# Norms of layers 0 and 1 on GpSimd in two passes over whole rows, their ramp in ScalarE's copy of the turned rows

## The chip, the cores and the metric

The kernel runs on one core of a Trainium2 chip. The metric is the time of one execution on the device in microseconds (us). The kernel before was run three times: the median is 1065.44 us, the lowest 1063.51, the highest 1066.78.

## The reference, cut to what matters

Sixteen graphs of 512 nodes with 128 features each pass through four graph layers, each behind a layer norm without weights and a ramp, and each added to its input:

```python
h = jnp.maximum(_layernorm(x, axis=-1), 0.0)      # (x - m) / sqrt(v + eps), then max(., 0)
x = x + _L0_gnn_ref(h, adj, L0_gnn_W, L0_gnn_a)   # attention over neighbours, one head
h = jnp.maximum(_layernorm(x, axis=-1), 0.0)
x = x + _L1_gnn_ref(h, adj, L1_gnn_W, L1_gnn_b, L1_gnn_a)   # the same with four heads
h = jnp.maximum(_layernorm(x, axis=-1), 0.0)
x = x + _L2_gnn_ref(h, adj, a0, a1, a2, a3, bias)  # edge kinds, sigmoid of h * a * h'
h = jnp.maximum(_layernorm(x, axis=-1), 0.0)
x = x + _L3_gnn_ref(h, adj, weight, w_ih, w_hh, b_ih, b_hh) # three rounds of a gated unit
```

In layers 0 and 1 h is used only through products with weights, so only the turned form of it (features on the partitions) is needed. Layers 2 and 3 use h also as it stands.

## The kernel before, in words

All arrays of a graph lie in SBUF as 128 partitions by 4 blocks (C = 4) by 128 features; a tile of 128x512 floats is a whole graph. Every step of a graph has a name. A_STEPS are layer 0, L_STEPS layer 1 (16 units n, v, q: masked maximum, exponential, transposition), B_STEPS layer 2, C_STEPS the three rounds of layer 3. Several graphs are in work at once: while one is in layers 2 and 3, the next is in layer 0 or 1. Each engine takes its own list of (graph, step), sorted by written times: BEGIN has the start of each of the four groups of steps for each graph, WHEN an offset for each step and engine (`in_order`, line 133). The order within an engine is fixed by these tables, and semaphores join the engines. Each engine works in order, so an instruction that waits holds all behind it.

A layer norm n goes like this:

- VectorE takes the sums (bn_stats, line 623), the moments (line 629), the negated mean (line 634) and variance plus eps (line 636; line 638 for layer 3).
- GpSimd raises the latter to the power -0.5 (line 363) and multiplies it with the negated mean into `shift` (line 365), both on 128x4 floats.
- ScalarE writes hn = relu(rstd * x + shift), in four activations of 128x128 (line 394), one for each block, since scale and shift are one number for each partition and block.
- TensorE turns the four blocks into a PSUM bank (`turn_rows`, line 936) and ScalarE copies that bank into hT in one activation of 128x512 (`copy_hT`, line 399).

On GpSimd's queue stand besides these only the two loads of adj of each graph (lines 371 and 379). In the middle of the run its order is: mean1 of graph g, mean0 of graph g+1, mean2 of g, the two loads, mean3 of g.

Other lines that are spoken of: 642 and 663 (masked maximum and logits of a unit on VectorE, operands spread, mask and probs in SBUF), 678 and 730 (the two masks, from adj in bf16), 739 (values out of PSUM), 796 and 802 (x2: the scaled product out of PSUM, then the addition of x1, both operands in SBUF), 870 (r_t times hid_n, both in SBUF), 885 (the new state, turned by TensorE on line 1142), 441 (ScalarE counts edges), 476 (ScalarE's copy avT, turned by TensorE on line 1049).

## Time and profile before

| | |
|---|---|
| median of 3 runs | 1065.44 us (1063.51 to 1066.78) |
| the profiled execution | 1066.04 us, span 1063.9 us |
| busy, share of the span | PE 90%, DVE 84%, ACT 81%, POOL 12% |
| mean granted TensorE clock | 0.967 of full speed |
| the chain that ended last | PE 52%, DVE 28%, ACT 10%, waiting for nothing shown 6%, POOL 3% |

PE is TensorE (PEld its weight loads), DVE VectorE, ACT ScalarE, POOL GpSimd. A row of the timeline has the start in us from the start of the span, the duration in us, the engine, the line of the kernel, the operation, the tiles (out<-in) with their shapes, and how many instructions were merged; in brackets stands how long the engine was idle in front of it and what ended that. The chain of work that ended last is followed back from the last instruction: at each step to what released it, or to the instruction before it on its engine.

### The profile page before, as it was taken

The numbers are of one execution on the slowest core, as the hardware profiler recorded it, in microseconds if no ns is written. First come the engines' busy times: TensorE is split into PE (matmuls) and PEld (weight loads), VectorE is DVE, ScalarE is ACT, GpSimd is POOL, SyncE is SP. The second block draws the span as 40 slices with busy tenths as digits, with TensorE's granted clock in tenths as the row PEclk, the third lists the DMA queues.
The fourth block names the chain that finished last, engine by engine and source line by source line (L and its number), as shares of the span: only waits on it lengthen the run. The fifth ranks groups of instructions, "written<-read, shape, count | busy, mean of one in ns | idle before, by whom it ended". The sixth has DMA issues, their size and how long they took to land.

```text
span 1063.9 us, 16086 instructions
## 1 busy us (share of the span) xinstructions
PE 954.6 (90%) x5024; PEld 609.6 (57%) x5024; DVE 892.3 (84%) x2710; ACT 864.0 (81%) x1860; POOL 132.6 (12%) x170
## 2 busy tenths in 40 slices
PE   4588998999989899999989899998989999998866
PEld 3455565666566566656556566656656665655443
DVE  5296989899898979899897989989897989979543
ACT  3367888979888897988888897988889798887742
POOL 1102011010202011020201201020201101010000
PEclk8558999999999999999999999999999999999989
DMA  2401204021210403121220402121030302111000
GB/s 72 109 1 39 72 11 109 11 61 52 68 51 14 106 11 77 44 60 51 56 64 10 110 11 60 60 61 51 15 105 11 79 31 61 50 40 51 1 11 10
DMA packets 42477, 52.32 MB, mean 49 GB/s; under 512 B 1296, under 2 KB 25872, under 8 KB 42384
## 3 DMA queue, kind: packets, MB, share of 16 engines
q0 software_dynamic: 16896, 25.17, 10.7%
q1 hardware_dynamic: 17040, 21.83, 6.5%
q10 hardware_dynamic: 8448, 4.20, 1.3%
q8 instruction: 44, 0.72, 0.3%
q14 instruction: 49, 0.40, 0.1%
HBM read 55.39 MB, written 4.19 MB: 56 GB/s over the span
## 4 chain that ended last, share of the span: by engine, by line
PE 52%; DVE 28%; ACT 10%; issue 6%; POOL 3%; DMA 0%; DVEq 0%; SPq 0%; ACTq 0%; POOLq 0%
PE l_bank L948 7%; DVE probs L642 6%; PE a_bank L981 6%; PE x_bank L1040 4%; PE a_bank L948 3%; PE h_bank L1102 3%; ACT hn L394 3%; PE r_bank L1102 3%; PE r_bank L1105 3%; DVE sess L843 3%; DVE sess L836 3%; PE h_bank L1105 3%; PE n_bank L1105 3%; DVE probs L663 3%; POOL rstd L363 2%
## 5 line engine op out<-in xcount | busy, mean ns | idle before, releaser
L663 DVE SCALAR_TENSOR_TENSOR probs<-spread,s_lift,probs 128x512 f32<-128x512 f32 x320 | 237.4, 747 | 4.0 <-DVE rmax L642 0.5
L642 DVE CUSTOM_DVE_ANT_0 probs<-spread,mask 128x512 f32<-128x512 f32 x320 | 211.8, 684 | 2.4 <-ACT spread L450 2.3
L363 POOL TENSOR_TENSOR rstd<-var_eps,power 128x4 f32<-128x4 f32 x64 | 88.0, 1375 | 882.5 <-DVE var_eps L636 603.0
L460 ACT ACTIVATE probs<-probs,shift_p 128x512 f32<-128x512 f32 x256 | 185.7, 725 | 5.7 <-DVE shift_p L659 5.7
L468 ACT ACTIVATE pT<-l_bank 128x512 f32<-128x512 f32 x256 | 151.8, 600 | 46.5 <-PE l_bank L948 46.3
L948 PEld LDWEIGHTS l_bank<-ident,probs 128*128 128x128 f32 x1024 | 124.3, 144 | 73.8 <-issue 46.0
L948 PE MATMUL l_bank<-ident,probs 128*128 128x128 f32 x1024 | 150.5, 278 | 6.1 <-ACT probs L460 5.1
L394 ACT ACTIVATE hn<-x,shift,rstd 128x128 f32<-128x128 f32 x192 | 80.5, 492 | 26.1 <-POOL shift L365 26.0
L1005 PE MATMUL l_bank<-hT,dst_rep 128*128 128x512 f32 x128 | 73.6, 658 | 12.1 <-ACT pT L468 8.5
L870 DVE SCALAR_TENSOR_TENSOR hid_n<-r_t,hid_n 128x512 f32<-128x512 f32 x48 | 33.1, 689 | 57.8 <-ACT r_t L518 57.8
L981 PE MATMUL a_bank<-values,pT 128*128 128x128 f32 x512 | 65.7, 286 | 0.7 <-ACT pT L428 0.7
L1088 PE MATMUL y_bank<-hn,sess 128*128 128x128 f32 x512 | 61.6, 278 | 4.2 <-DVE sess L843 4.1
L1088 PEld LDWEIGHTS y_bank<-hn,sess 128*128 128x128 f32 x512 | 58.4, 192 | 11.9 <-DVE sess L843 11.9
L981 PEld LDWEIGHTS a_bank<-values,pT 128*128 128x128 f32 x512 | 63.0, 202 | 2.0 <-ACT pT L428 2.0
L1040 PE MATMUL x_bank<-pT,values 128*32 128x512 f32 x512 | 58.2, 595 | 0.7 <-ACT pT L468 0.7
L450 ACT ACTIVATE spread<-l_bank 128x512 f32<-128x512 f32 x64 | 38.4, 600 | 23.4 <-PE l_bank L1005 23.4
L948 PEld LDWEIGHTS a_bank<-ident,probs 128*128 128x128 f32 x256 | 29.9, 149 | 44.5 <-ACT pT L428 35.8
L948 PE MATMUL a_bank<-ident,probs 128*128 128x128 f32 x256 | 44.4, 300 | 9.7 <-ACT probs L423 5.6
L460 ACT ACTIVATION_READ_ACCUMULATOR probs<-probs,shift_p 128x1 f32 x256 | 51.8, 202 | 0.0
L1105 PE MATMUL r_bank<-aggT,gi_w 128*128 128x512 f32 x96 | 49.4, 596 | 0.0
L1105 PE MATMUL h_bank<-aggT,gi_w 128*128 128x512 f32 x96 | 49.1, 593 | 0.0
L1105 PE MATMUL n_bank<-aggT,gi_w 128*128 128x512 f32 x96 | 49.1, 593 | 0.0
(175 smaller groups left out, 1956.5 us busy)
## 6 DMA issues: line engine op xcount, KB each, us to landing
adjt_i<-in_adj_t SPq DMA_DIRECT2D x16, 1024.0 KB, 5.2
edges<-in_adj POOLq DMA_DIRECT2D x16, 1024.0 KB, 5.9
adj_h<-in_adj POOLq DMA_DIRECT2D x16, 512.0 KB, 7.7
xin<-in_x SPq DMA_DIRECT2D x16, 256.0 KB, 2.9
out<-out_sb ACTq DMA_DIRECT2D x16, 256.0 KB, 3.8
weights_sb<-in_weights SPq DMA_DIRECT2D x1, 840.0 KB, 4.7
```

The lines of the kernel that those rows point to most:

```text
L363: g.tensor_tensor(rstd[n][:], var_eps[n][:], power[:], op=ALU.pow).then_inc(pool_step[n], 1)
L394: s.activation(hn[n][:, c, :], rows[:, c, :], ACT.Relu, bias=shift[n][:, c:c + 1], scale=rstd[n][:, c:c + 1]).then_inc(hn_ready[n], 1)
L460: s.activation(row, row, ACT.Exp, bias=shift_p[:, head, c:c + 1], accum_out=den[:, head, c:c + 1]).then_inc(probs_ready, 1)
L468: s.activation(pT[:, head - 1, :, c * P:(c + 1) * P], l_banks[unit % 2][:, :].rearrange("p (j i) -> p j i", j=C), ACT.Copy).then_inc(pT_co ...
L642: return v.tensor_tensor_reduce(out=row, in0=spread_row, in1=mask, scale=1.0 / LIFT, scalar=-3e38, op0=ALU.subtract, op1=ALU.max, accum_ou ...
L663: v.scalar_tensor_tensor(row, spread_row, source, row, ALU.min, ALU.subtract, reverse1=True).then_inc(ready, 1)
L948: last = t.transpose(dst[:, j * P:(j + 1) * P], row[:, j * P:(j + 1) * P], ident[:])
L981: last = t.matmul(a_bank[:, c * P:(c + 1) * P], pT0[:, j, c * P:(c + 1) * P], values0[:, j, :], start=(j == 0), stop=(j == C - 1))
L1005: t.matmul(l_banks[head % 2][:, :], dst_rep[:, head, :], hT[1][:, :], start=True, stop=True).then_inc(dst_ready, 1)
L1040: last = t.matmul(x_bank[h * HD:(h + 1) * HD, :], values1[:, j, h * HD:(h + 1) * HD], pT[:, h, j, :], start=(j == 0), stop=(j == C - 1), s ...
L1088: last = t.matmul(y_bank[:, c * P:(c + 1) * P], sess[:, j, c * P:(c + 1) * P], hn[2][:, j, :], start=False, stop=(j == C - 1), skip_group_ ...
L1105: t.matmul(bank[:, :], gi_w[:, layer, gate * D:(gate + 1) * D], aggT[:, :], start=start, stop=True).then_inc(gi_ready, 1)
```

## The change

For layers 0 and 1 the normalization moves from ScalarE to GpSimd. GpSimd subtracts the mean from the whole 128x512 tile (the mean is read from `moments`, spread over each block's 128 features), waits for its own result, and multiplies the whole tile with rstd, spread in the same way. The ramp goes to the copy of the turned rows: `copy_hT` uses Relu in place of Copy for n < 2. For these two layers the negated mean on VectorE and the product for `shift` on GpSimd fall away, the step names norm0_0 to norm0_3 (norm1_0 to norm1_3) become one step norm0 (norm1), and `turn_rows` waits for one pass in place of four. GpSimd's new steps stand directly behind mean0 and mean1 of the same graph. The tables WHEN lose the entries of the steps that fell away; the order of all that stays is the same on every engine. Layers 2 and 3 are as before.

The diff, without the tables:

```diff
--- before.py
+++ after.py
@@ -20,9 +20,9 @@
 PLAIN = 1024.0
 
 
-A_STEPS = (["stats0", "aggr0", "mean0"] + [f"norm0_{c}" for c in range(4)] + ["rows0", "mask0", "dst0", "src0", "values0"] + [f"m{c}" for c in range(4)]
+A_STEPS = (["stats0", "aggr0", "mean0"] + ["norm0"] + ["rows0", "mask0", "dst0", "src0", "values0"] + [f"m{c}" for c in range(4)]
            + ["u0", "top0", "u1", "t0", "below0", "u2", "t1", "max0", "u3", "t2", "t3", "den0", "rden0"] + [f"sum0_{c}" for c in range(4)] + ["x1"])
-L_STEPS = (["stats1", "aggr1", "mean1"] + [f"norm1_{c}" for c in range(4)] + ["count", "rows1", "mask1", "dst1", "edges", "values1"]
+L_STEPS = (["stats1", "aggr1", "mean1"] + ["norm1"] + ["count", "rows1", "mask1", "dst1", "edges", "values1"]
            + [f"n{c}" for c in range(4)] + ["dst2"]
            + [step for n in range(16)
...
@@ -279,6 +276,7 @@
         stats_ready = [sem(f"stats_ready{n}") for n in range(NORMS)]
         pool_step = [sem(f"pool_step{n}") for n in range(NORMS)]
         ln_ready = [sem(f"ln_ready{n}") for n in range(NORMS)]
+        centred = [sem(f"centred{n}") for n in range(2)]
         hn_ready = [sem(f"hn_ready{n}") for n in range(NORMS)]
         hT_ready = [sem(f"hT_ready{n}") for n in range(NORMS)]
         hT_copied = [sem(f"hT_copied{n}") for n in range(NORMS)]
@@ -362,7 +360,18 @@
                 pool.wait_ge(stats_ready[n], p.count(1, 1))
                 g.tensor_tensor(rstd[n][:], var_eps[n][:], power[:], op=ALU.pow).then_inc(pool_step[n], 1)
                 pool.wait_ge(pool_step[n], p.count(1, 1))
-                g.tensor_tensor(shift[n][:], minus_mean[n][:], rstd[n][:], op=ALU.mult).then_inc(ln_ready[n], 1)
+                if n >= 2:
+                    g.tensor_tensor(shift[n][:], minus_mean[n][:], rstd[n][:], op=ALU.mult).then_inc(ln_ready[n], 1)
+
+            def norm(p, n, rows):
+
+                if p.before().exists():
+                    pool.wait_ge(hT_ready[n], p.before().count(1, 1))
+                g.tensor_tensor(hn[n][:, :, :], rows, moments[n][:, :, 0:1].to_broadcast([P, C, D]),
+                                op=ALU.subtract).then_inc(centred[n], 1)
+                pool.wait_ge(centred[n], p.count(1, 1))
+                g.tensor_tensor(hn[n][:, :, :], hn[n][:, :, :], rstd[n][:, :].unsqueeze(2).to_broadcast([P, C, D]),
+                                op=ALU.mult).then_inc(hn_ready[n], 1)
 
             def load_adj(p):
                 if p.before().exists():
@@ -379,6 +388,10 @@
                     g.dma_start(edges[:, p.graph % 2, :, :], rows(adj, p.graph)).then_inc(edges_loaded[p.graph % 2], 16)
                 if step[:4] == "mean":
                     deviation(p, int(step[4]))
+                if step == "norm0":
+                    norm(p, 0, xin[:, p.graph % 2, :, :])
+                if step == "norm1":
+                    norm(p, 1, x1[:, p.graph % 2, :, :])
 
             load_adj(Place(0))
             for graph, step in in_order("gpsimd", G):
@@ -396,13 +409,11 @@
 
             def copy_hT(p, n, src):
                 act.wait_ge(hT_ready[n], p.count(1, 1))
-                s.activation(hT[n][:, :], src[:, :], ACT.Copy).then_inc(hT_copied[n], 1)
+                s.activation(hT[n][:, :], src[:, :], ACT.Relu if n < 2 else ACT.Copy).then_inc(hT_copied[n], 1)
 
             def step_a(p, step):
                 prev = p.before()
-                if step[:5] == "norm0":
-                    norm(p, 0, int(step[6]), xin[:, p.graph % 2, :, :])
-                elif step == "rows0":
+                if step == "rows0":
                     copy_hT(p, 0, a_bank)
                 elif step == "dst0":
                     act.wait_ge(dst0_ready, p.count(1, 1))
@@ -430,9 +441,7 @@
 
             def step_l(p, step):
                 prev = p.before()
-                if step[:5] == "norm1":
-                    norm(p, 1, int(step[6]), x1[:, p.graph % 2, :, :])
-                elif step == "rows1":
+                if step == "rows1":
                     copy_hT(p, 1, l_bank0)
                 elif step == "count":
                     act.wait_ge(adj_loaded, p.count(16, 16))
@@ -631,7 +640,8 @@
 
             def deviation_of(n, chain):
                 chain.wait()
-                v.tensor_scalar(minus_mean[n][:, :], moments[n][:, :, 0], -1.0, None, ALU.mult)
+                if n >= 2:
+                    v.tensor_scalar(minus_mean[n][:, :], moments[n][:, :, 0], -1.0, None, ALU.mult)
                 if n < NORMS - 1:
                     last = v.tensor_scalar(var_eps[n][:, :], moments[n][:, :, 1], EPS, None, ALU.add)
                 else:
@@ -931,7 +941,8 @@
                     t.matmul(bk[:, 0:3 * D], gate_wt_sb[i], w_iht_sb[:], start=True, stop=True).then_inc(pe_w, 1)
 
             def turn_rows(p, n, dst):
-                pe.wait_ge(hn_ready[n], p.count(C, C))
+                passes = C if n >= 2 else 1
+                pe.wait_ge(hn_ready[n], p.count(passes, passes))
                 for c in range(C):
                     last = t.transpose(dst[:, c * P:(c + 1) * P], hn[n][:, c, :], ident[:])
                 last.then_inc(hT_ready[n], 1)
```

## Rows read from the trace of the kernel before

**Rows 1.** The page, busy us (share of the span) and instructions by engine.
```profile
PE 954.6 (90%) x5024; PEld 609.6 (57%) x5024; DVE 892.3 (84%) x2710; ACT 864.0 (81%) x1860; POOL 132.6 (12%) x170
```

**Rows 2.** Busy time by stretch: A, then B; columns in the first line.
```profile
core 0: us, PE busy (x) PEld busy (x) DVE busy (x) ACT busy (x) POOL busy (x), PEclk, DMA share, GB/s
398.00:424.10 26.10, 23.96 (x121) 15.72 (x120) 25.68 (x79) 20.12 (x44) 3.51 (x5) 1.00 0.30 66
424.10:458.65 34.55, 33.31 (x196) 21.05 (x195) 29.25 (x89) 33.38 (x74) 5.72 (x6) 1.00 0.13 43
```

**Rows 3.** Waits, 205.8 to 874.1 us: total us, times, longest.
```profile
DVE hid_n L870 <- ACT r_t L518: 28.6, 11, 3.2
...
PE x_bank L936 <- ACT hn L394: 9.7, 13, 0.8
```

**Rows 4.** Groups of instructions: busy us, mean ns, idle us before them.
```profile
L394 ACT ACTIVATE hn<-xin,shift,rstd 128x128 f32<-128x128 f32 x64 | 26.2, 482 | 4.7 <-POOL shift L365 4.7
```

**Rows 5.** Timeline of one period, 448 to 466 us, all engines.
```profile
448.75 1.01 POOL L363 TENSOR_TENSOR rstd<-var_eps,power 128x4 f32<-128x4 f32 x1 [22.84 <-DVE var_eps L636]
...
451.71 0.69 DVE L870 SCALAR_TENSOR_TENSOR hid_n<-r_t,hid_n 128x512 f32<-128x512 f32 x1 [3.04 <-ACT r_t L518]
...
452.44 1.66 ACT L394 ACTIVATE hn<-x,shift,rstd 128x128 f32<-128x128 f32 x4
...
454.40 2.58 POOL L363 TENSOR_TENSOR rstd<-var_eps,power 128x4 f32<-128x4 f32 x1 [4.36 <-DVE var_eps L636]
...
456.15 0.69 DVE L885 SCALAR_TENSOR_TENSOR state<-keep,n_t 128x512 f32<-128x512 f32 x1
...
456.92 0.66 PE L936 MATMUL l_bank<-ident,hn 128*128 128x128 f32 x4
...
457.42 0.60 PE L1142 MATMUL h_bank<-ident,state 128*128 128x128 f32 x4
...
459.38 0.69 DVE L802 TENSOR_TENSOR x<-x 128x512 f32<-128x512 f32 x1
...
459.94 1.64 ACT L394 ACTIVATE hn<-xin,shift,rstd 128x128 f32<-128x128 f32 x4
...
463.50 1.38 POOL L363 TENSOR_TENSOR rstd<-var_eps,power 128x4 f32<-128x4 f32 x1 [6.24 <-DVE var_eps L636]
...
464.80 0.60 PE L936 MATMUL a_bank<-ident,hn 128*128 128x128 f32 x4
```

**Rows 6.** Groups of instructions on GpSimd: fills and the select.
```profile
L358 POOL TENSOR_SCALAR_AFFINE_SELECT ident<-ident 128x128 f32<-128x128 f32 x1 | 0.3, 287 | 0.2 <-POOL ones_h L356 0.2
...
L353 POOL MEMSET ident<- 128x128 f32 x1 | 0.2, 202 | 0.0
...
L354 POOL MEMSET power<- 128x4 f32 x1 | 0.1, 98 | 0.0
```

**Rows 7.** Timeline, GpSimd beside three VectorE instructions, two places.
```profile
40.64 0.86 DVE L623 BATCH_NORM_STATS2 stats<-xin 128x6 f32<-128x128 f32 x4
40.81 1.01 POOL L363 TENSOR_TENSOR rstd<-var_eps,power 128x4 f32<-128x4 f32 x1 [34.13 <-DVE var_eps L636]
...
41.84 0.66 DVE L730 TENSOR_SCALAR mask<-adj_h 128x2048 bf16<-128x2048 bf16 x1
41.91 0.65 POOL L365 TENSOR_TENSOR shift<-minus_mean,rstd 128x4 f32<-128x4 f32 x1
...
100.74 0.42 DVE L739 TENSOR_TENSOR values<-l_bank,b_rows 128x256 f32<-128x256 f32 x1
100.91 1.01 POOL L363 TENSOR_TENSOR rstd<-var_eps,power 128x4 f32<-128x4 f32 x1 [6.52 <-DVE var_eps L636]
```

**Rows 8.** Timeline, a period of the other kind, 576 to 583 us.
```profile
578.21 1.38 POOL L363 TENSOR_TENSOR rstd<-var_eps,power 128x4 f32<-128x4 f32 x1 [6.19 <-DVE var_eps L636]
...
581.33 0.69 DVE L802 TENSOR_TENSOR x<-x 128x512 f32<-128x512 f32 x1
```

**Rows 9.** Timeline, norm 1 of the first graph, 40 to 47 us.
```profile
44.38 1.09 PE L936 MATMUL l_bank<-ident,hn 128*128 128x128 f32 x4 [6.47 <-ACT hn L394]
...
46.13 0.57 ACT L399 ACTIVATE hT<-l_bank 128x512 f32<-128x512 f32 x1
```

131 rows, old and new, of the table WHEN are left out of this document.

## Prediction

> **What bounds the kernel now.** I read the page's totals first. TensorE is busy for 90% of the span, VectorE for 84%, ScalarE for 81% and GpSimd for 12% [rows 1]. So the idle engine is the one that gets the work, but the share alone doesn't say what relief on ScalarE is worth. For that I read a table by stretch. In the middle of the run one graph leaves every 60.8 us (mean of 13 periods, 145.8 to 936.2 us), and each period falls into two stretches. Stretch A runs from the addition that makes x2 (line 796) to the variance of layer 3: 26.10 us, of which VectorE is busy 25.68. Stretch B is the rest: 34.55 us, TensorE busy 33.31, ScalarE 33.38, VectorE only 29.25 [rows 2]. The chain of work that ended last has VectorE in A and TensorE in B, and four more periods look alike. So a period is VectorE's work in A plus TensorE's work in B. ScalarE is very busy in B, but it is TensorE that has no gap there: of its 1.24 idle us, about 0.9 is the wait for the rows of layer 3's norm (9.7 us in 11 periods [rows 3]), which the change doesn't touch.
>
> **What is removed.** On ScalarE 128 activations of 128x128 at about 0.48 us each [rows 4], each started before the one in front of it ends: the four of norm 1 take 1.66 us at the end of B, and the four of norm 0 1.64 near the start of A [rows 5]. Norm 1 is done at 454.1 us and its transposes start at 456.92; norm 0 is done at 461.6 and its transposes start at 464.80 [rows 5]. TensorE waits for neither in the steady periods. What is behind them on ScalarE (gate activations, the count, the copies of avT and hT) comes at most a fraction earlier, since it waits for TensorE, which is full. Gain: at most 1.24 - 0.9, some 0.4 us a period, if all waits of B went, 5 us in 13; I take 0.1 a period, 1 us. On VectorE 32 small instructions (minus_mean) go, all in B, where VectorE waits anyway (28.6 us in 11 periods for r_t [rows 3]): nothing. GpSimd's product for shift goes, 32 times 0.2 us or a little more. The copy of the turned rows keeps its instruction with another function: taken as nothing, as both kinds read the same bank; if it cost 0.1 us more the copy for layer 1 would have to be paid, 1.6 us at most.
>
> **What is added: the price of a pass.** GpSimd gets 64 passes over 128x512 floats, each reading two operands. No row of before shows one. GpSimd fills 128x128 in 0.202 us and 128x4 in 0.098, which is 0.84 ns an element of a row for a write; the affine select, which reads once and writes once, takes 0.287 for 128 elements, 1.52 ns [rows 6]. A read is thus about 0.68 ns, and two reads and a write about 2.2 ns: 0.2 + 508 x 2.2 = 1.32 us a pass. Lower end: both operands at the price of one, 0.2 + 508 x 1.52 = 0.97. Upper end: the whole price twice, 1.75. I take 1.32, the sum of the parts. The two passes with their two hand-overs of 0.08 end 2.80 us after the power.
>
> The Trainium skill has a price of its own (GPSIMD Engine Reference, section 3.1): a two-input pass over 2048 floats takes 4497 ns. By it I would estimate 1.2 to 1.3 us for 512, and a sum about 1 us lower; no row here shows it.
>
> **Do they come in time?** Norm 1: the power ends at 449.76, the passes at 452.56, or 0.7 later if a VectorE instruction cuts in; the transposes start at 456.92. Norm 0: the power ends at 456.98, the passes at 459.8; the transposes start at 464.80 [rows 5]. Both earlier than ScalarE delivers now. Behind norm 1 on GpSimd's queue stands the power of the next graph's norm 0, four or more us later; behind norm 0 the power of layer 2, at 463.50 [rows 5], and only then the two loads of adj. None of them is moved.
>
> **What they collide with.** The power reads four elements of two tiles. Beside bn_stats (one operand from SBUF) it takes 1.01 us, and beside line 739 (one operand from PSUM) also 1.01. The shift product, 0.20 us alone, takes 0.65 when the mask of line 730 runs in front of it, and so ends just after that mask [rows 7]. The power at 454.40 takes 2.58: VectorE works through a mask and instructions with two SBUF operands without a gap, and GpSimd gets in only before the last [rows 5]. So GpSimd stands still while VectorE runs a mask or two SBUF operands. That VectorE stands still when GpSimd is the first, no row shows: GpSimd's reads of four elements are too short. I take it that the block holds both ways, and for the whole pass.
>
> The Trainium skill says so (SBUF — State Buffer, section "Who interferes with whom"): the pair of ports that VectorE and GpSimd share is an exclusive lock, and "whoever issues first" holds it for the whole instruction. The trace agrees with the half in which VectorE is first; for the other half it is silent.
>
> Place 1, in A, where VectorE is the bound. The addition of line 802 reads x1 and x2 from SBUF. In front of it the power for norm 0 ends at 456.98 and it starts at 459.38, 2.40 us later [rows 5]; in the other kind of period 579.59 and 581.33, 1.74 us later [rows 8]. Read in the same way, 7 of the 13 periods have 2.36 to 2.41 and 6 have 1.51 to 1.88. The second pass starts 1.48 after the power, mostly ahead of the addition, and ends at 2.80: it holds VectorE for 0.40 us in each of the seven, 2.8 us, and for 1.1 on average in the six, 6.6 us. Together 9.4. The 0.4 us a period by which VectorE isn't busy in A [rows 2] may swallow some: I take 0.25 a period, 3 us. Left: 6.4.
>
> Place 2, in B. Line 870 (r_t and hid_n, both in SBUF) starts 0.9 to 2.16 us after the power of norm 1, 1.95 in the period shown (449.76 to 451.71). Eight times it meets the first pass for 0.2 to 0.5 us, five times the second for 0.6 to 0.9. What hides it is the slack of the state: made at 456.84, read by TensorE at 457.42 [rows 5], 0.58 us less a hand-over of 0.05. Only the five go over, by some 0.3: 1.5 us.
>
> Place 3, the first graph. TensorE waits 6.47 us for norm 1, which starts at 44.38 [rows 9]. The first pass waits for the mask until 42.50, and the two passes end at 45.2, some 0.9 late. But the copy behind the transposes starts only at 46.13, since it stands behind the count on ScalarE, and the count now runs 1.6 us earlier; the copy then starts at about 46.45. That is 0.3; with the constants of VectorE at 6 to 10 us, which norm 0 may hold up to 1 us, I take 0.7.
>
> **The sum.** 6.4 + 1.5 + 0.7 - 1.0 = +7.6 us. The profiled execution has 1066.04 us, 2.14 beyond its span of 1063.9, and gives 1073.6; it lies 0.6 above the median of 1065.44. On the median: 1073.0 us. With a pass of 0.97 the two are over before the addition in the seven and cost 2.3 us in the six, which A swallows: 1065. With 1.75 it meets the addition by 1.25 us in seven periods, and the first pass alone reaches it in the six; line 870 goes over the slack in most periods, some 8 us: together +18, 1084.
>
> **Rivals.**
> - VectorE isn't held: it wins every time, or GpSimd's reads slip between its instructions. For it: no VectorE instruction of before is stretched beside GpSimd. Against: none ever stood behind a long read. Then only the 1 us of relief and 0.7 at the start are left: 1065.
> - The relief on ScalarE counts: it is as full as TensorE in B [rows 2], and with 1.66 us a period less in its queue what follows could reach TensorE sooner. Against: TensorE's waits for ScalarE in B are small. At most 0.4 a period: 1060.
> - The pass holds VectorE in places that I count as free, slower than forecast: it costs 1.75 us, or also stops instructions with one SBUF operand. The place is the same, lines 796 to 802 at the head of A; it decides from a pass of about 1.5 us on. 1084.
> - The forecast itself is slower than before; the point from which it bites is (2.40 - 0.16) / 2 = 1.12 us a pass in the seven periods, 0.8 in the six.
>
> **Chances.** Forecast 0.53, VectorE not held 0.26, relief counts 0.12, heavy case 0.09. A measurement of this kernel tells 0.3% (3.2 us) from no change. Faster by over that: 0.11, most of the relief case. Within: 0.31, the unheld case with the low end of the forecast. Slower: 0.58. The range leaves out the best of the relief case and the end of the heavy one: 1062 to 1083.
>
> **What would show it.** Right: GpSimd's passes at 1.2 to 1.4 us where VectorE is silent; line 802, 0.69 us now, at 1.1 to 1.8 or starting late after line 796; line 870 the same in some periods; stretch A longer by 0.3 to 1 us, B by less than 0.3; TensorE's and ScalarE's spans in B as they are. Wrong: line 802 stays at 0.69 and A at 26 us (VectorE isn't held), or B shrinks with ScalarE (relief). Wrong too if a transposition of norm 0 or 1 waits for GpSimd, or if the power of layer 2 starts late.

## The result and the profile after

The changed kernel takes 1067.89 us, the median of 13 runs (1066.74 to 1070.35), against 1065.49 for 13 runs of the kernel before: a ratio of 1.0027, 95% interval 1.0018 to 1.0036. It is 2.4 us slower, where 7.6 was forecast. The profiled execution took 1067.27 us, with a span of 1065.5.

The page's totals of the kernel after, to be read against [rows 1]:

```profile
PE 948.3 (89%) x5008; PEld 606.6 (57%) x5024; DVE 900.0 (84%) x2678; ACT 818.7 (77%) x1732; POOL 191.9 (18%) x202
```

ScalarE lost 45.3 us of work and GpSimd gained 59.3. VectorE has 32 instructions fewer and yet is busy 7.7 us longer. That is the trail to follow.

Stretches A and B of one period, as in [rows 2] (same columns):

```profile
399.17:424.99 25.82, 23.44 (x117) 15.44 (x117) 25.39 (x77) 18.30 (x40) 4.37 (x5) 1.00 0.27 65
424.99:459.72 34.73, 33.48 (x198) 21.35 (x198) 29.49 (x89) 32.48 (x70) 8.85 (x8) 1.00 0.14 44
```

A is no longer than before, B is. In this period A went from 26.10 to 25.82 and B from 34.55 to 34.73. Over the 13 periods the sum of A went from 336.82 to 336.77 and that of B from 453.14 to 454.56.

GpSimd's groups in the kernel after (busy us, mean ns), and the spread of one of them (minimum, median, maximum in ns):

```profile
L373 POOL TENSOR_TENSOR hn<-hn,rstd 128x512 f32<-128x512 f32 x32 | 35.4, 1105 | 2.5
L370 POOL TENSOR_TENSOR hn<-x,moments 128x512 f32<-128x512 f32 x16 | 17.1, 1072 | 1.3
```
```profile
L370 POOL TENSOR_TENSOR hn<-xin,moments x16: 1042/1044/1161, 6.1 to 885.5; 128x512 f32<-128x512 f32 x16
```

A pass is 1.04 us where nothing disturbs it, not 1.32. Longer ones are those that VectorE itself stops, as at 43.12 us below.

Line 870 is now 880, 802 is 812, 885 is 895, 1142 is 1153, 796 is 806, 363 is 361, 936 is 947, 399 is 412, 476 is 485, 1049 is 1060. Durations of two lines of VectorE in the kernel after; before, no instruction of either took more than 0.693 us:

```profile
L880 DVE SCALAR_TENSOR_TENSOR hid_n<-r_t,hid_n x48: 679/692/1559, 136.0 to 1056.8; 128x512 f32<-128x512 f32 x48
...
L812 DVE TENSOR_TENSOR x<-x x16: 679/692/1214, 99.4 to 1004.5; 128x512 f32<-128x512 f32 x16
```

The timeline of one period of the kernel after, 389 to 401 us, to be read against [rows 5]:

```profile
389.48 1.01 POOL L361 TENSOR_TENSOR rstd<-var_eps,power 128x4 f32<-128x4 f32 x1 [23.50 <-DVE var_eps L646]
...
390.56 1.04 POOL L370 TENSOR_TENSOR hn<-x,moments 128x512 f32<-128x512 f32 x1
...
391.68 1.04 POOL L373 TENSOR_TENSOR hn<-hn,rstd 128x512 f32<-128x512 f32 x1
391.77 1.50 DVE L880 SCALAR_TENSOR_TENSOR hid_n<-r_t,hid_n 128x512 f32<-128x512 f32 x1 [2.37 <-ACT r_t L527]
...
395.20 2.58 POOL L361 TENSOR_TENSOR rstd<-var_eps,power 128x4 f32<-128x4 f32 x1 [2.47 <-DVE var_eps L646]
...
396.95 0.69 DVE L895 SCALAR_TENSOR_TENSOR state<-keep,n_t 128x512 f32<-128x512 f32 x1
...
396.98 0.66 PE L947 MATMUL l_bank<-ident,hn 128*128 128x128 f32 x4
...
397.69 0.66 PE L1153 MATMUL h_bank<-ident,state 128*128 128x128 f32 x4
397.86 1.05 POOL L370 TENSOR_TENSOR hn<-xin,moments 128x512 f32<-128x512 f32 x1
...
398.99 1.04 POOL L373 TENSOR_TENSOR hn<-hn,rstd 128x512 f32<-128x512 f32 x1
399.17 0.69 DVE L806 TENSOR_TENSOR x<-y_bank,rden 128x512 f32<-128x512 f32 x1 [1.53 <-PE y_bank L1060]
...
399.90 0.69 DVE L812 TENSOR_TENSOR x<-x 128x512 f32<-128x512 f32 x1
```

Three readings. Line 880 starts just behind the second pass of norm 1 and takes 1.50 us: it gets going only when that pass is over. The state then ends at 397.64, and TensorE turns it at 397.69, 0.71 us behind the turn of norm 1 (0.50 in [rows 5], and 0.49 in this very period of the kernel before), so it waited 0.2 us. And the passes of norm 0 end at 400.03, hardly later than line 812 starts (399.90), which keeps its 0.69.

The other kind of period, to be read against [rows 8]:

```profile
579.26 1.38 POOL L361 TENSOR_TENSOR rstd<-var_eps,power 128x4 f32<-128x4 f32 x1 [4.38 <-DVE var_eps L646]
...
580.72 1.04 POOL L370 TENSOR_TENSOR hn<-xin,moments 128x512 f32<-128x512 f32 x1
...
581.85 1.04 POOL L373 TENSOR_TENSOR hn<-hn,rstd 128x512 f32<-128x512 f32 x1
582.36 1.07 DVE L812 TENSOR_TENSOR x<-x 128x512 f32<-128x512 f32 x1
```

Here the addition starts 1.72 us after the power's end and is held for 0.38. Only two of the 13 periods show it by more than 0.05 us (0.38 and 0.52).

Two more places matter in B. In the first, norm 0's pass gets in ahead of the instruction that makes the state (line 895) and holds it for 0.73 us. In the second, line 880 had been held for 0.87, and the delay travels through ScalarE: its n_t gate waits 0.58 us for VectorE's hid_n, the count stands behind the gate, the copy avT (line 485) behind the count, and TensorE turns avT on line 1060:

```profile
334.91 1.16 POOL L370 TENSOR_TENSOR hn<-xin,moments 128x512 f32<-128x512 f32 x1
...
335.21 1.42 DVE L895 SCALAR_TENSOR_TENSOR state<-keep,n_t 128x512 f32<-128x512 f32 x1
```
```profile
760.34 0.72 ACT L535 ACTIVATE n_t<-hid_n,gate_b 128x512 f32<-128x512 f32 x1 [0.58 <-DVE hid_n L884]
...
762.96 0.57 ACT L485 ACTIVATE avT<-x_bank 128x512 f32<-128x512 f32 x1
...
763.68 0.63 PE L1060 MATMUL y_bank<-ident,avT 128*128 128x128 f32 x4
```

The first graph, whose start the change touches twice. In the kernel before the four copies of the constants took 0.68 us and the first transposes started at 9.53:

```profile
6.06 1.04 POOL L370 TENSOR_TENSOR hn<-xin,moments 128x512 f32<-128x512 f32 x1
...
6.66 1.76 DVE L591 COPY a_heads<-weights_sb 32x2 f32<-32x2 f32 x4
7.18 1.04 POOL L373 TENSOR_TENSOR hn<-hn,rstd 128x512 f32<-128x512 f32 x1
...
11.15 1.06 PE L947 MATMUL a_bank<-ident,hn 128*128 128x128 f32 x4
```

And its norm 1, to be read against [rows 9]:

```profile
43.06 0.66 DVE L740 TENSOR_SCALAR mask<-adj_h 128x2048 bf16<-128x2048 bf16 x1
43.12 1.49 POOL L370 TENSOR_TENSOR hn<-x,moments 128x512 f32<-128x512 f32 x1
43.63 1.01 DVE L646 TENSOR_SCALAR var_eps<-moments 128x4 f32<-128x4 f32 x1
44.70 1.04 POOL L373 TENSOR_TENSOR hn<-hn,rstd 128x512 f32<-128x512 f32 x1
...
45.88 1.08 PE L947 MATMUL l_bank<-ident,hn 128*128 128x128 f32 x4 [6.69 <-POOL hn L373]
...
47.00 0.60 ACT L412 ACTIVATE hT<-l_bank 128x512 f32<-128x512 f32 x1 [12.47 <-PE l_bank L947]
```

Both sides of the block stand in these lines. The pass at 43.12 is long (1.49) because the mask is in front of it; then VectorE's 128x4 instruction at 43.63, 0.16 us else, takes 1.01 because the pass is in front of that.

### The profile page after: what moved, and what is told of

Its sections match the earlier page's. It is cut to its first block, busy times and chain, and to the rows that moved or that the text cites. A ratio compares the mean times of both kernels' runs of the same rounds, so it can differ in the third digit from the quotient of the medians.

```text
span 1065.5 us, 15972 instructions
## 1 busy us (share of the span) xinstructions
PE 948.3 (89%) x5008; PEld 606.6 (57%) x5024; DVE 900.0 (84%) x2678; ACT 818.7 (77%) x1732; POOL 191.9 (18%) x202
## 4 chain that ended last, share of the span: by engine, by line
PE 48%; DVE 32%; ACT 10%; issue 6%; POOL 3%; DMA 0%; DVEq 0%; SPq 0%; ACTq 0%; POOLq 0%
DVE probs L652 7%; PE a_bank L992 6%; PE l_bank L959 6%; PE x_bank L1051 4%; PE a_bank L959 3%; PE h_bank L1113 3%; DVE probs L673 3%; DVE sess L846 3%; PE r_bank L1113 3%; DVE sess L853 3%; DVE stats L632 3%; PE r_bank L1116 3%; PE h_bank L1116 2%; PE n_bank L1116 2%; ACT hn L407 2%
## 5 line engine op out<-in xcount | busy, mean ns | idle before, releaser
L361 POOL TENSOR_TENSOR rstd<-var_eps,power 128x4 f32<-128x4 f32 x64 | 84.0, 1313 | 824.7 <-DVE var_eps L646 546.9
L469 ACT ACTIVATE probs<-probs,shift_p 128x512 f32<-128x512 f32 x256 | 185.7, 725 | 5.9 <-DVE shift_p L669 5.9
L880 DVE SCALAR_TENSOR_TENSOR hid_n<-r_t,hid_n 128x512 f32<-128x512 f32 x48 | 38.5, 801 | 58.6 <-ACT r_t L527 58.6
L407 ACT ACTIVATE hn<-x,shift,rstd 128x128 f32<-128x128 f32 x128 | 53.4, 483 | 17.1 <-POOL shift L364 17.1
L520 ACT ACTIVATE aggT<-n_bank 128x512 f32<-128x512 f32 x32 | 19.1, 598 | 53.0 <-PE n_bank L1131 53.0
L434 ACT ACTIVATE probs<-probs,shift_p 128x512 f32<-128x512 f32 x64 | 46.3, 731 | 4.4 <-DVE shift_p L669 4.4
```

The lines of the kernel that those rows point to most:

```text
L361: g.tensor_tensor(rstd[n][:], var_eps[n][:], power[:], op=ALU.pow).then_inc(pool_step[n], 1)
L407: s.activation(hn[n][:, c, :], rows[:, c, :], ACT.Relu, bias=shift[n][:, c:c + 1], scale=rstd[n][:, c:c + 1]).then_inc(hn_ready[n], 1)
L469: s.activation(row, row, ACT.Exp, bias=shift_p[:, head, c:c + 1], accum_out=den[:, head, c:c + 1]).then_inc(probs_ready, 1)
```

## The experiments

The theory is the prediction's: a pass holds every VectorE instruction with two SBUF operands that comes behind it, in three places. Rivals: VectorE isn't held at all; the loss comes from the start alone; the relief of ScalarE is what moves the time. Here are all kernels in one table. "First x2" is the start of line 796 for the first graph, A and B are summed over the 13 periods, "tail" runs from the end of layer 3's variance of the last graph to the end of the last arithmetic instruction (the span goes on for 2.3 us, for the store of the result); these come from one profile each. "Held" is the time over 0.69 us, with its count, of line 802 and of line 870. Medians and ratios are against the kernel before in the same series.

| kernel | first x2 | A | B | tail | 802 held | 870 held | median (before) | ratio, 95% |
|---|---|---|---|---|---|---|---|---|
| before | 97.82 | 336.82 | 453.14 | 39.15 | 0 | 0 | 1065.49 | |
| after | 98.69 | 336.77 | 454.56 | 38.75 | 0.95 (3) | 5.42 (10) | 1067.89 (1065.49) | 1.0027, 1.0018 to 1.0036 |
| relief_only | 92.05 | 336.33 | 452.49 | 42.42 | 0 | 0 | 1059.80 (1065.86) | 0.9941, 0.9929 to 0.9954 |
| passes_only | 99.01 | 339.00 | 453.26 | 42.38 | 4.00 (10) | 2.67 (10) | 1068.37 (1065.86) | 1.0031, 1.0013 to 1.0049 |
| fills_only | 96.90 | 335.82 | 452.95 | 39.07 | 0 | 0 | 1068.49 (1065.86) | 1.0020, 1.0002 to 1.0037 |
| norm0_only | 99.03 | 337.82 | 453.31 | 40.50 | 1.91 (6) | 0 | 1069.28 (1065.86) | 1.0028, 1.0017 to 1.0038 |
| norm1_only | 96.47 | 336.42 | 453.88 | 38.96 | 0 | 5.41 (10) | 1064.47 (1064.01) | 0.9998, 0.9988 to 1.0009 |
| third_pass | 97.93 | 339.63 | 454.01 | 38.78 | 4.57 (8) | 5.42 (10) | 1071.80 (1064.01) | 1.0075, 1.006 to 1.009 |
| after_add | 98.61 | 337.66 | 453.85 | 42.37 | 0 | 5.47 (10) | 1072.59 (1064.01) | 1.0072, 1.0058 to 1.0086 |
| one_operand | 96.43 | 336.27 | 452.60 | 43.50 | 0 | 0 | 1064.86 (1064.01) | 1.0004, 0.9995 to 1.0014 |
| graph0_scalar | 98.16 | 337.17 | 454.97 | 42.93 | 0.90 (2) | 5.27 (9) | 1069.44 (1065.61) | 1.0033, 1.0015 to 1.005 |
| graph0_one_operand | 94.40 | 337.22 | 452.89 | 40.44 | 0 | 0 | 1065.31 (1065.61) | 0.9998, 0.9987 to 1.001 |
| third_pass_norm1 | 98.69 | 336.99 | 454.39 | 39.92 | 1.43 (4) | 5.51 (10) | 1070.38 (1065.61) | 1.005, 1.0033 to 1.0068 |
| by_block | 96.02 | 336.82 | 452.57 | 43.57 | 1.15 (9) | 1.76 (11) | 1068.00 (1065.61) | 1.0012, 0.9999 to 1.0025 |
| before_again | 98.00 | 336.76 | 453.08 | 39.11 | 0 | 0 | 1066.11, one run | |
| after_again | 98.05 | 336.90 | 454.37 | 40.44 | 0.95 (3) | 5.43 (10) | 1068.60, one run | |

How far can a column be trusted? The last two rows repeat the two kernels:

> The kernel before, profiled once more. Theory (what differs between executions of one kernel is the granted clock before 150 us and in the last 40, not the steady part): the 13 periods from 155 to 945 us sum to 790.0 us within 0.5; the start up to the first addition of x2 and the stretch behind the last norm may differ by 1 to 3 us with the clock. Rival (the steady part itself moves by 1 us or more from execution to execution, so the sums say nothing): a sum off by 1 us or more.

> The changed kernel, profiled once more. Theory: the 13 periods sum to 791.3 us within 0.5, 1.4 over before, with line 870's held instructions at 5.4 us in all and line 802's at 0.9; start and end go with the clock. Rival: the sum is off by 1 us or more and the held instructions lie elsewhere.

The sum A + B is 789.96 and 789.84 before, 791.33 and 791.27 after: the same within 0.12 us, so the 13 periods cost 1.4 us, and the held instructions repeat too. The first x2 moves by up to 0.6 us and the tail by 1.7 between executions of one kernel. The steady stretch is read from these sums; the ends of the span only by their mechanism, and medians that differ by 3 us or less with care. This caution is needed: of the twelve altered kernels, only passes_only and third_pass_norm1 have a median inside the range that the theory gave in advance. third_pass and one_operand miss it by up to 0.2 us, the other eight by 1 us or more. What follows therefore goes by the sums over the periods and by the held instructions.

### The two halves of the change

**relief_only.** TensorE turns the rows as they are; the norms fall away:

```diff
-            def norm(p, n, rows):
...
-                    last = t.transpose(dst[:, c * P:(c + 1) * P], hn[n][:, c, :], ident[:])
+                    rows = (xin, x1)[n][:, p.graph % 2] if n < 2 else hn[n]
+                    last = t.transpose(dst[:, c * P:(c + 1) * P], rows[:, c, :], ident[:])
```

> The changed kernel without its 32 pairs of passes: norms 0 and 1 are left out (TensorE turns the rows as they are once the power is there), the ramp stays in the copy. Theory (the passes hold VectorE, relief on ScalarE is worth nothing): 1064 to 1066 us, stretch B as long as before. Rival 1 (the relief is worth 3 us or more and the passes cost twice what shows): 1060 to 1062 us. Rival 2 (all of the loss is at the start, VectorE's constants held by norm 0 of graph 0): 1064 to 1066 as well, but then the periods of the changed kernel are as long as these.

The median fell by 6 us, more than any case foresaw. In the profile the first x2 is 5.8 us earlier, since the first graph, where all engines wait for it, has no norms to wait for. In the 13 periods A lost 0.49 and B 0.65: the relief is 1.1 us. The rival that relief counts has no more than that to live on, and this kernel, not before, is the base for what the passes cost: A + 0.44 and B + 2.07 in the kernel after.

**passes_only.** The kernel before, with the same two passes into a tile that nobody reads:

```diff
+            def passes(p, n, rows):
+                wide = extra[:, :].rearrange("p (c d) -> p c d", c=C)
...
+                g.tensor_tensor(wide, rows, moments[n][:, :, 0:1].to_broadcast([P, C, D]),
+                                op=ALU.subtract).then_inc(centred[n], 1)
+                pool.wait_ge(centred[n], p.count(1, 1))
+                g.tensor_tensor(wide, wide, rstd[n][:, :].unsqueeze(2).to_broadcast([P, C, D]),
+                                op=ALU.mult).then_inc(scaled_ready[n], 1)
```

> The kernel before with the 32 pairs of passes added on GpSimd, into a tile that nobody reads; ScalarE keeps its norms. Theory: the loss of the change, 2 to 4 us over before, with line 870 and a few others stretched by up to 0.9 us. Rival 1: 5 us or more over before, since the relief is missing. Rival 2: 1 to 2 us, all of it before 100 us.

No engine reads what these passes write. Only guards against overwriting wait for passes of earlier graphs, and the profile shows no such wait but two of loads of x, for neither of which VectorE then waits. Still the kernel is slower. Line 802 is held in 10 of its 16, 4.0 us in all; A grows by 2.18. Here shift's product comes first, so the passes end some 0.14 us later, and the gaps between the power and line 802 are close to those that the prediction read: 1.51 to 1.87 in six periods, 2.05 to 2.36 in seven. The place and the mechanism are as forecast; the size hangs on tenths of a microsecond. That A grows by 1.8 less than the holds looks like the part that A was to swallow, but it isn't an even 0.25 a period: of the four largest holds (0.74, 0.65, 0.51 and 0.47) the periods grew by 0.43, 0.86, 0.51 and 0.04.

**fills_only.** The same, with two writes of the same length that read nothing:

```diff
-                g.tensor_tensor(wide, rows, moments[n][:, :, 0:1].to_broadcast([P, C, D]),
-                                op=ALU.subtract).then_inc(centred[n], 1)
+                g.memset(wide, 1.0).then_inc(centred[n], 1)
```

> As the kernel with passes added, but each pass is a fill of 1.04 us that reads nothing. Theory (it is GpSimd's reads that hold VectorE's second SBUF operand): line 870 and line 802 stay at 0.69 us and the time at before's, 1065 to 1066; only VectorE's masks and copies may still be held. Rival (GpSimd holds VectorE whatever it does): as with the passes, 2 to 4 us over before.

Groups and timeline of fills_only:

```profile
L379 POOL MEMSET fills<- 128x1128 bf16 x32 | 33.7, 1052 | 1.9
...
L826 DVE TENSOR_TENSOR x<-x 128x512 f32<-128x512 f32 x16 | 11.0, 689 | 0.4
```
```profile
6.55 2.51 DVE L601 COPY a_heads<-weights_sb 32x2 f32<-32x2 f32 x4
...
701.01 1.04 POOL L379 MEMSET fills<- 128x1128 bf16 x1
...
701.21 0.69 DVE L826 TENSOR_TENSOR x<-x 128x512 f32<-128x512 f32 x1
```

GpSimd is as busy as with the passes, but neither line is held, and A + B is 1.2 us below before (why below, I can't say). Line 802 starts within a fill 6 times, with up to 0.83 us of it left, and line 870 14 times, with up to 0.51 left; none takes over 0.69. A GpSimd that is merely busy and writes thus doesn't hold them: it takes a pass that reads. Some instructions with one operand are held by a fill also: the constants' copies take 2.51 us, a 128x4 one 1.07, and one mask 1.50 in place of 0.69. The median doesn't follow the sums: the 12 runs fall into two groups, 1063.2 to 1064.5 and 1068.5 to 1070.7. What makes the groups isn't in the 13 periods of the profile that I have, which is of a run of the lower group. passes_only and graph0_scalar fall into two groups in the same way (1066.1 to 1068.9 and 1071.8 to 1074.4; 1064.3 to 1066.0 and 1069.1 to 1073.1), so a median there depends on how many runs fell into each.

**norm0_only** and **norm1_only.** The change for one of the two layers, the other as before:

```diff
-                g.tensor_tensor(shift[n][:], minus_mean[n][:], rstd[n][:], op=ALU.mult).then_inc(ln_ready[n], 1)
+                if n != 0:
+                    g.tensor_tensor(shift[n][:], minus_mean[n][:], rstd[n][:], op=ALU.mult).then_inc(ln_ready[n], 1)
...
+                if step == "mean0":
+                    whole(p, 0, xin[:, p.graph % 2, :, :])
```

> Only norm 0 is moved to GpSimd, norm 1 stays on ScalarE. Theory: the start costs 0.9 us, place 1 (line 802 in A) almost nothing since a pass takes 1.04 us and not 1.32: 1066 to 1067 us. Forecast's view (place 1 carries most): 1067 to 1068 and norm 1 alone would cost nothing.

> Only norm 1 is moved to GpSimd, norm 0 stays on ScalarE. Theory: line 870 is held by up to 0.9 us as in the changed kernel, and of that about 1 us in 13 periods goes over the slack of the state in B; A stays; the start loses some 0.5 us. 1066 to 1068 us. Rival (the two norms' costs add up to the change's): 1065 us, since norm 0 alone already costs about all of it.

The medians are again of little help: norm0_only is 2.3 us above the range expected, norm1_only 1.5 below. With norm 0 alone A grows by 1.0 and B by 0.17, six additions are held; with norm 1 alone A loses 0.4 and B gains 0.74, ten of line 870 are held. One hold of each kernel shows how close this is. Norm0_only:

```profile
154.13 1.38 POOL L364 TENSOR_TENSOR rstd<-var_eps,power 128x4 f32<-128x4 f32 x1 [5.82 <-DVE var_eps L648]
155.59 1.04 POOL L372 TENSOR_TENSOR hn<-xin,moments 128x512 f32<-128x512 f32 x1
156.72 1.04 POOL L375 TENSOR_TENSOR hn<-hn,rstd 128x512 f32<-128x512 f32 x1
...
157.36 0.95 DVE L814 TENSOR_TENSOR x<-x 128x512 f32<-128x512 f32 x1
```

The gap from the power's end (155.51) to the addition is 1.85 us, and 0.26 is lost. The six gaps 1.58, 1.66, 1.80, 1.84, 1.85 and 1.95 go with 0.52, 0.44, 0.29, 0.25, 0.26 and 0.15: 2.11 less the gap within 0.03 each time. In the kernel after, where norm 1 holds line 870 as well, the same periods have 1.57, 2.05, 1.72, 2.31, 2.30 and 2.40, and only three are held. So moving norm 1 too takes holds away from norm 0's passes: three of the six gaps grew beyond the point from which it bites, and a fourth nearly to it. It isn't the delay of line 870 that does this. In relief_only nothing is held, and the same periods, in the same order, have 2.02, 2.05, 2.31, 2.31, 2.31 and 2.40 (one_operand within 0.04); in passes_only line 870 is held while ScalarE keeps its norms, and they have 1.51 to 1.87. What moves the gaps is that norm 1 leaves ScalarE (and with it go its negated mean on VectorE and its shift on GpSimd). Its passes, as far as the comparison goes, work the other way: with them two of the six are back at 1.57 and 1.72, and these two are the ones that pay in the kernel after. Norm1_only shows the same with norm 0 on ScalarE: 1.50 and 1.64 there, 1.98 to 2.33 in the other four.

In sum over the periods, A and B together, norm 0 costs 1.2, norm 1 0.3 and both 1.4, with the relief in each; only the share of A and B is another (A + 1.0 and - 0.4 alone, 0 together).

### The dose

**third_pass.** One more pass ahead of norm 0's two:

```diff
+                if n == 0:
+                    g.tensor_tensor(extra[:, :, :], rows, moments[n][:, :, 0:1].to_broadcast([P, C, D]),
+                                    op=ALU.subtract).then_inc(extra_done, 1)
+                    pool.wait_ge(extra_done, p.count(1, 1))
```

> The changed kernel with a third pass in front of norm 0's two, into a tile that nobody reads: the passes end 3.25 us after the power and not 2.1. Theory (line 802 is held exactly as long as a pass still runs when it comes): in the 7 periods with a gap of 2.3 to 3.8 us it is held by up to 1 us, in the others by what is left of the second pass, and A grows by 0.3 to 0.7 us a period, 4 to 8 us over the changed kernel: 1072 to 1076. Rival (VectorE's gaps in A swallow it): below 1070.

A is 2.86 us longer than in the kernel after, B 0.55 shorter, and line 802 is held 4.57 us in place of 0.95. The median is 7.8 us over before, of which the periods hold 3.7. One period of third_pass shows why the periods don't lose more:

```profile
396.51 2.58 POOL L363 TENSOR_TENSOR rstd<-var_eps,power 128x4 f32<-128x4 f32 x1 [2.48 <-DVE var_eps L652]
...
399.17 1.04 POOL L373 TENSOR_TENSOR extra<-xin,moments 128x512 f32<-128x512 f32 x1
...
400.29 1.04 POOL L376 TENSOR_TENSOR hn<-xin,moments 128x512 f32<-128x512 f32 x1
...
401.21 0.69 DVE L818 TENSOR_TENSOR x<-x 128x512 f32<-128x512 f32 x1
...
401.41 1.39 POOL L379 TENSOR_TENSOR hn<-hn,rstd 128x512 f32<-128x512 f32 x1
```

The addition comes in the seam between two passes, goes first, and the third pass waits (1.39 for 1.04). So the point isn't how long the norm lasts but in which pass the addition falls.

**third_pass_norm1.** The same line with `if n == 1`.

> The changed kernel with a third pass in front of norm 1's two. Theory (the slack of the state is 0.5 us, one held instruction costs what goes over it): line 870 is held in nearly every period by 0.3 to 0.9 us, as now; the five periods in which it came after the passes now pay too, and norm 0's power comes later against line 802: 0 to 3 us over the changed kernel, far less than norm 0's third pass (A grew by 2.9 us): 1068 to 1071. Rival (a pass costs the same wherever it stands): 1072 or more.

Line 870 is held 5.51 us against 5.42, and A + B is 791.38 against 791.33: line 870 meets the second of three passes where it met the second of two, and starts 0.07 us behind it (0.09 in the kernel after). A further pass behind the one that holds costs nothing here. The median is 4.8 us over before, and that is not in the periods: in the profile the tail is 1.2 longer than in the kernel after, and the rest isn't accounted for.

**after_add.** Norm 0's passes wait for the addition:

```diff
+                if n == 0 and p.before(2).exists():
+                    pool.wait_ge(x2_ready, p.before(2).count(1, 1))
```

> The changed kernel, but norm 0's passes wait for the addition of line 802 of the graph in layer 2. Theory: line 802 is back at 0.69 us everywhere, the passes lie beside bn_stats and operands from PSUM, the transposes of norm 0 still don't wait; A is shorter by what two held additions cost, 0.5 to 1 us: 1066.5 to 1067.5. Rival (the two held additions were no cost in the period): as the changed kernel, 1067.9. Rival 2 (norm 0 now comes too late for its transposes): 1070 or more.

The median, 1072.59, is as high as rival 2 has it, but not for its reason: no transposition of norm 0 waits. Line 802 is free, but A is 0.9 longer than in the kernel after and A + B the same (791.51). The passes now fall on the masked maxima, of which seven are held for 1.86 us; before, all of them took at most 0.69. The hold was moved, not removed. That the median is 4.7 over that of the kernel after isn't in the periods either; the tail of this profile is 3.6 longer.

**one_operand.** Each norm in four instructions with both numbers as scalars, so that only one operand is a row:

```diff
-                g.tensor_tensor(hn[n][:, :, :], rows, moments[n][:, :, 0:1].to_broadcast([P, C, D]),
-                                op=ALU.subtract).then_inc(centred[n], 1)
...
+                for c in range(C):
+                    last = g.tensor_scalar(hn[n][:, c, :], rows[:, c, :], moments[n][:, c, 0:1], rstd[n][:, c:c + 1],
+                                           ALU.subtract, ALU.mult)
```

> The changed kernel, but GpSimd makes a norm in four instructions of 128x128, each (row - mean) * rstd with two scalars of a partition, so one operand of 512 elements is read in place of two times two. Theory: some 0.3 us an instruction, 1.2 us a norm in place of 2.1; line 870 and line 802 are held for 0.3 us at most: 1065 to 1066 us, and the start loses less. Rival (an instruction costs by its start, 0.5 us or more): 2 us a norm and no gain, 1067 to 1068.

One_operand's own GpSimd instructions, and its addition beside them:

```profile
L371 POOL TENSOR_SCALAR hn<-xin,moments,rstd x64: 790/798/1333, 6.2 to 883.2; 128x128 f32<-128x128 f32 x64
```
```profile
395.38 2.87 POOL L371 TENSOR_SCALAR hn<-xin,moments,rstd 128x128 f32<-128x128 f32 x3
...
396.88 0.71 DVE L811 TENSOR_TENSOR x<-x 128x512 f32<-128x512 f32 x1
```

An instruction takes 0.79 us where 0.3 was expected, so a norm lasts 3.2 us and more, longer than two passes, and lies across the addition. Lines 802 and 870 start within such an instruction 26 times, with up to 1.21 us of it left, and none is lengthened by more than 0.02. One state is held for 0.14 us, and at the start two tiny instructions for 0.2 together. A + B is 788.87, 1.1 below before, and A and B each within 0.12 of relief_only: that is the relief, at next to no price. The form of GpSimd's instruction decides, not its length. These instructions read SBUF too, so reading by itself isn't enough to hold VectorE; what in the form does it (one row operand for two, the scalars, or the pace) isn't separated here. Its median is within 0.1% of before all the same.

**by_block.** Each pass in four instructions of 128x128, so that VectorE can cut in:

```diff
+                for c in range(C):
+                    last = g.tensor_tensor(hn[n][:, c, :], rows[:, c, :],
+                                           moments[n][:, c, 0:1].to_broadcast([P, D]), op=ALU.subtract)
```

> The changed kernel with each pass cut into four instructions of 128x128 on the same operands. Theory (the hold lasts as long as one instruction reads): line 870 and line 802 are held by 0.3 us at most, steady periods 1 to 2 us shorter in all than the changed kernel's: 1065 to 1067, unless four starts make a pass so long that the transposes wait. Rival (VectorE is kept out for the whole row of instructions): as the changed kernel or more, 1068 to 1070.

The quarter passes take 0.40 us each (median), no hold is over 0.26, and together they are 2.91 us on the two lines against 6.37. B is 2 us below the kernel after. What is lost is the rest of the instruction in progress, so shorter instructions lose less each time. The median doesn't show it: 1068.00, 1 us above the range expected, with 4.8 us more in the tail of its profile than in the kernel after.

### The start

**graph0_scalar.** The first graph's norms stay on ScalarE:

```diff
+                    if p.graph == 0:
+                        for c in range(C):
+                            norm(p, 0, c, xin[:, 0, :, :])
```

> The changed kernel, but the two norms of the first graph stay on ScalarE as before. Theory (norm 0 of the first graph holds VectorE's copies of the constants): the first transposes start at 9.6 us and not at 11.2, the time falls by 1 to 2 us to 1066 to 1067, the steady periods stay. Rival (the start doesn't matter, since other waits cover it): as the changed kernel, 1067.9.

The first transposes start at 9.62 again (11.15 and 11.29 after; 9.53 and 10.16 before), so it was norm 0 of the first graph that moved them. The constants' copies, 1.76 us in the kernel after, are back at 0.71. No gain follows in time: 1069.44. First x2 is 0.5 earlier only, and the tail is 42.93.

**graph0_one_operand.** The same together with one_operand, for all later graphs.

> The first graph's norms on ScalarE, all others on GpSimd with one operand and two scalars in four instructions of 128x128. Theory: no place holds VectorE any more, and the relief of ScalarE is left: 13 periods 1.1 us shorter than before, start as before: 1062.5 to 1064, at the edge of what can be told from before. Rival (relief is nothing): 1064 to 1065.5.

The median is 1065.31 against 1065.61, level with the kernel before and above the 1062.5 to 1064 expected. Four states are held for 0.13 us each, so "no place" was too strong. Of the kernels that still compute the norms, none is measurably faster than the kernel before.

## Why the prediction was right or wrong

**The bound: right.** A follows VectorE and B follows TensorE. With no norms for layers 0 and 1 at all (relief_only), B is only 0.05 us a period shorter.

**The relief: right in sum.** Forecast were 1.0 us, all of it in B; relief_only has 1.1, of which 0.5 in A.

**That a pass holds VectorE: right.** It was taken without a row, and every kernel with passes shows it. The rival "not held" is out: its 1065 is what one_operand gives (1064.86), not this change. The Trainium skill (SBUF — State Buffer, "Who interferes with whom") has this exclusive lock with the first comer as its owner; the seam in third_pass and the two long instructions at 43.12 and 43.63 agree. One_operand shows a limit: 26 times VectorE comes second to a GpSimd instruction that reads SBUF, and it isn't stopped.

**The price of a pass: wrong, and the step that failed.** The forecast of +7.6 rests on place 1 with 6.4 us, and place 1 on this price. 1.32 was taken, the sum of a read, a read and a write; it is 1.04, near the lower end of 0.97, which had two operands at the price of one. The passes end 2.25 us after the power, not 2.80, and VectorE goes on 0.14 before their recorded end. The Trainium skill's table (GPSIMD Engine Reference, section 3.1), by which I would have estimated 1.2 to 1.3, is nearer, yet also high for 512 elements here.

**Place 1: wrong by that price.** Forecast 9.4 held, 6.4 left. The rule (2.11 us less the gap) holds to a few hundredths in norm0_only. In the gaps read before, it gives nothing in the seven periods at 2.36 and over, and for the six (mean 1.71) 0.40 each, 2.4 us. Measured are 0.95, and A + 0.44 over the relief alone; A, which was to grow by 0.3 to 1 us a period, is as long as before. The rest of the difference is a second error: the gaps were held fixed, while the relief alone moves all six to 2.02 or more. The 0.25 us a period that A was to swallow isn't borne out either: in the two periods held for 0.38 and 0.52, A is 0.38 and 0.52 longer than in relief_only, and the other eleven are each up to 0.08 shorter.

**Place 2: near in sum, by another path.** Forecast: 1.5 us from five periods in which line 870 goes over the slack of the state. Measured: ten holds, 5.42 us, each up to 0.87, and B + 2.07 over the relief alone. Holds of about 0.1 cost nothing. The six of 0.81 and more lengthen B by 0.02 to 0.53 us, 1.2 together, but in only one of them is the state late for TensorE. In that one and in four others the copy avT comes late, through ScalarE's queue: TensorE turns it 1.03 to 1.43 us behind norm 1's rows, against 0.93 in every period of relief_only. The prediction had no such path. The other 0.7 isn't line 870's: norm 0's first pass holds the state itself (line 885) for 0.73 in three periods, and these are 0.16 to 0.30 longer.

**Place 3: not settled.** Forecast 0.7; the first x2 came 0.87 later in one pair of profiles and 0.05 in the other, so an agreement in size would be luck. The first transposes are late by 1.6 and 1.1 in the two pairs. The copy behind norm 1 is late by 0.9 in one and by nothing in the other, where 0.3 was reckoned.

**What did not happen.** No transposition of norm 0 or 1 waits for GpSimd in the middle of the run, and the copy with the ramp costs what it did (0.58 to 0.60).

**The sum.** From the profiles: first x2 + 0.87, up to the first of the 13 periods - 0.30, the periods + 1.37, behind them - 0.40; together 1.54, and the span grew by 1.6. The repeated pair gives + 0.05, 0, + 1.43 and + 1.35. So 1.4 us of the slowdown are shown to be the holds less the relief. The other 1.0 of the median isn't in the periods, and its cause isn't settled. The likeliest case was put too far out; with 1.04 in its own sum it would have come out near + 2.1 (place 1 at 2.4 less the 0.25 that A swallows in each of six periods, 0.9; then 1.5, 0.7 and - 1.0). That is an afterthought and no forecast, and its closeness to the measured 2.4 is partly luck, since the gaps, the swallowed part and the path in B were wrong as well.

## What to carry to other kernels

Before work goes to an idle GpSimd, look for which VectorE instructions start within it: here a GpSimd instruction that reads two row operands stopped those with two SBUF operands until 0.14 us before its recorded end, while one with a row and two scalars per partition (0.79 us for 128x128) stopped them for 0.14 us at most. Bound the cost by gaps, from the release of GpSimd to the start of the next two-operand instruction, at both ends of the price, and treat those gaps as moving: whether a pass costs nothing or most of its length is decided by tenths of a microsecond. And follow a late instruction through every engine that waits for it: here the delay of one VectorE instruction reached TensorE by way of ScalarE's queue. Put down a median's last 3 us to a mechanism only when a stage sum in the profile shows the same.

## What the hardware showed that I had not expected

The last stretch has the same work in each kernel and takes from 39 to 43 us. Windows over it, for the kernel before, the kernel after, passes_only and, from a little before it, after_again (columns as above):

```profile
1022.50:1061.60 39.10, 26.27 (x76) 14.06 (x76) 12.89 (x19) 13.88 (x23) 1.21 (x2) 0.91 0.00 0
```
```profile
1024.50:1063.10 38.60, 25.87 (x76) 13.87 (x76) 12.89 (x19) 13.87 (x23) 1.19 (x2) 0.90 0.00 0
```
```profile
1026.00:1069.00 43.00, 29.49 (x76) 16.21 (x76) 12.88 (x19) 13.87 (x23) 1.20 (x2) 0.84 0.00 1
```
```profile
1022.50:1062.90 40.40, 27.13 (x75) 15.04 (x76) 13.66 (x28) 13.87 (x23) 1.21 (x2) 0.86 0.00 0
```

VectorE and ScalarE are busy for the same time (after_again's window begins with nine small instructions more); TensorE's 76 instructions (one record is missing in after_again) take 25.87 to 29.49 us, at a mean granted clock (the column before the last two) of 0.91 down to 0.84, between its levels of 1.2 and 2.4 GHz. The stretch of the start, 36 to 98 us, differs too: 0.66 before, 0.71 after and 0.66 in after_again, 0.65 in after_add. From 150 to 940 us it is 1.00 in the kernel before, the kernel after and after_add. Two executions of the same kernel after lie 0.90 and 0.86 apart in the tail, so the kernel's text doesn't fix it. after_add, 4.7 us slower than the kernel after at equal period sums, has 0.84 in its tail. What sets the level remains open, and with it whether the change itself shifts it.
